# Mixture-of-experts block: four banks for the dense tile, its sums between the last rotations, W2's pieces inside it

## What is computed

```python
# layer 1: causal sums of exponentials, then a small gate
q, k = rope((x @ Wq.T).bf16), rope((x @ Wk.T).bf16)
scores = q @ k.T / 16
o = where(causal, exp(scores), 0).sum(-1)          # one number per row
x = layernorm(x + relu(o @ fc1_w.T + fc1_b) @ fc2_w.T + fc2_b)
# layer 2: three routers, 12 experts each, top 3 by softmax
xa = x @ P_w.T
C1, C2, C3 = (top3_softmax(xa @ U.T) for U in (U1, U2, U3))
h = gelu(sum(C1[:, e] * (x @ W1[e].T) for e in range(12)))
y = sum(C2[:, e] * (h @ W2[e].T) for e in range(12)) + C3 @ b2
x = layernorm(x + y)
```

## Time and profile before

| | us |
|---|---|
| median of 3 runs | 312.19 |
| lowest, highest | 311.31, 315.37 |
| the profiled execution | 311.88 |
| its span | 310.0 |
| PE busy | 273.9 (88%) |
| DVE busy | 249.2 (80%) |
| ACT busy | 164.0 (53%) |
| GpSimd (POOL) busy | 145.2 (47%) |

### The profile page before, as it was taken

The page is one execution under the profiler, slowest core; times in us unless marked ns, Lnnn a source line. Parts: engine busy times, 40 slices in busy tenths (PEclk is TensorE's granted clock), DMA queues, the critical chain, the costliest instruction groups (busy, mean ns, idle before and its releaser), DMA issues.

```text
span 310.0 us, 6417 instructions
## 1 busy us (share of the span) xinstructions
PE 273.9 (88%) x2028; PEld 196.9 (64%) x2030; DVE 249.2 (80%) x728; ACT 164.0 (53%) x341; POOL 145.2 (47%) x315
## 2 busy tenths in 40 slices
PE   7997999979791985999998998998998999899980
PEld 5443455434351553778887787787777878688870
DVE  0378689999979265488999999999999989987872
ACT  1247746755662116406854854854854956654430
POOL 0200017999999611225356256256256353374421
PEclk9999999997998598699999999999999999999997
DMA  8998999950000000000010010011000010110111
GB/s 235 416 393 246 169 169 207 146 71 0 0 3 1 0 0 0 2 2 19 19 30 23 18 30 26 17 27 30 18 24 30 20 32 26 32 32 21 37 34 38
DMA packets 19211, 20.50 MB, mean 66 GB/s; under 512 B 1620, under 2 KB 18408, under 8 KB 18664
## 3 DMA queue, kind: packets, MB, share of 16 engines
q1 hardware_dynamic: 18456, 19.13, 26.2%
q10 hardware_dynamic: 720, 0.93, 1.0%
HBM read 15.83 MB, written 4.19 MB: 65 GB/s over the span
## 4 chain that ended last, share of the span: by engine, by line
PE 40%; DVE 27%; POOL 14%; issue 8%; SPq 4%; DMA 4%; ACT 2%; DVEq 0%; POOLq 0%
PE bank L922 31%; DVE early L1287 9%; POOL W L406 5%; DMA W<-in_w2T 4%; POOL wtmp L403 4%; POOL W L405 3%; PE bank L760 2%; PE bank L808 2%; DVE early L1336 2%; SPq L333 2%; DVE st L1331 2%; DVE top L1156 2%; DVE x1T L1146 1%; DVE stats L1135 1%; DVE zrest L1171 1%
## 5 line engine op out<-in xcount | busy, mean ns | idle before, releaser
L922 PE MATMUL bank<-W,x1T 128*128 (+1 forms) x630 | 79.4, 281 | 8.5 <-DVE early L1287 5.0
L922 PE MATMUL bank<-W,early 128*128 (+1 forms) x630 | 74.5, 273 | 6.0 <-DVE early L1336 5.4
L922 PEld LDWEIGHTS bank<-W,x1T 128*128 128x128 f16 x630 | 61.4, 101 | 21.9 <-DVE early L1287 7.2
L1287 DVE SCALAR_TENSOR_TENSOR early<-bank,Csel,early 128x256 f32<-128x256 f32 x124 | 59.7, 482 | 14.2 <-PE bank L922 9.7
L922 PEld LDWEIGHTS bank<-W,early 128*128 128x128 f16 x630 | 59.5, 98 | 17.4 <-DVE early L1336 7.0
L760 PE MATMUL bank<-early,wqk 128*128 128x512 f32 x128 | 61.3, 611 | 2.4 <-ACT qk L551 1.8
L760 PEld LDWEIGHTS bank<-early,wqk 128*128 128x128 f32 x128 | 22.6, 193 | 22.9 <-issue 20.3
L672 ACT ACTIVATE early<-early 128x256 f32<-128x256 f32 x32 | 13.3, 417 | 45.0 <-DVE early L1287 44.7
L509 POOL TENSOR_SCALAR ve<-mv 128x1 f32<-128x1 f32 x32 | 7.3, 228 | 59.6 <-DVE mv L1332 58.9
L551 ACT ACTIVATE qk<-bank 128x512 bf16<-128x512 f32 x32 | 18.9, 594 | 30.6 <-PE bank L760 30.4
L1062 DVE TENSOR_TENSOR xcos<-qk,cb 128x1024 bf16<-128x1024 bf16 x16 | 12.0, 749 | 18.6 <-ACT qk L551 18.5
(11 more groups left out here) (117 smaller groups left out, 454.5 us busy)
## 6 DMA issues: line engine op xcount, KB each, us to landing
early<-in_xT SPq DMA_DIRECT2D x16, 256.0 KB, 7.8
xs<-in_x SPq DMA_DIRECT2D x32, 128.0 KB, 7.9
out<-early SPq DMA_DIRECT2D x32, 128.0 KB
W<-in_w1T SPq DMA_DIRECT2D x1, 2048.0 KB, 11.8
W<-in_w2T SPq DMA_DIRECT2D x1, 2048.0 KB, 12.4
W<-in_w1T SPq DMA_DIRECT2D x1, 1024.0 KB, 7.2
W<-in_w2T SPq DMA_DIRECT2D x1, 1024.0 KB, 14.1
wqk<-in_wqkT ACTq DMA_DIRECT2D x1, 512.0 KB, 3.7
```

What stands on the lines that cost most here:

```text
L922: mm = pe.matmul(where[:, 0:DIM], lhs(hx, c), w, start=(k == 0), stop=(k == 5))
L1287: dve.scalar_tensor_tensor(sums, bank[place[n]][:, 0:DIM], c, before, ALU.mult, ALU.add)\
```

## The change

The list place starts at bank 2 and goes round four banks from product 0. The last chunk's scores (7) get the banks HGT and MISC. On PE the products of tile 0 are dealt out anew between the last scores, and tile 1's first products (mixture(1, 0)) stand ahead of bias(0, 0), x1_transpose(2, 0) and bias(0, 1). On DVE the sums of tile 0 begin between rope(7, 0) and rope(7, 1), route_ids(0) ahead of them. W2's shared pieces (n = 4 to 7) leave chunks 6 and 7 on ACT and DVE and stand in the dense tile. On GpSimd weights_of(0) and C3_split(0) stand ahead of a W piece in chunk 7, and the last two pieces after select_of(0) and norm_scale(2). On ACT gelu(0) stands ahead of x1_high(2, 0) and bias_copy(0, 0), and begin(1) inside the dense tile.

```diff
@@ -173,6 +173,8 @@
         bank = [ps(f"bank{i}", [P, 512]) for i in range(8)]
         PROJ, SCORE, HGT, ROWS, XPOSE, MISC = (0, 1), (2, 3), 4, 5, 6, 7
         RING, HT = 4, 4
+        LAST_SCORE = (HGT, MISC)
         WARM = 28
         Z = GT * NR * NE
         KEPT = 10
@@ -284,7 +286,7 @@
 
 
 
-        place = [n % 2 if n < NE else n % RING for n in range(len(taker))]
+        place = [(n + SCORE[0]) % RING for n in range(len(taker))]
         before = [max((k for k in range(n) if place[k] == place[n]), default=None) for n in range(len(taker))]
 
         def last(t, m):
@@ -301,6 +303,9 @@
             n = 4 * (c - 3) + j
             if 0 <= n < len(EARLY):
                 aux(*EARLY[n])
+        def score_bank(n):
+            return bank[(SCORE if n < SPC * (NCH - 1) else LAST_SCORE)[n % 2]]
 
         def group(g):
             return 0 <= g < NG
@@ -490,14 +495,19 @@
             piece = 0
             for c in range(NCH):
                 for j in range(4):
+                    if (c, j) == (NCH - 1, 1):
+                        continue
                     early_aux(c, j, early)
+                    if (c, j) == (NCH - 1, 0):
+                        early_aux(c, 1, early)
+                        C3_split(0)
                     if c >= 4:
                         w_piece(piece)
                         piece += 1
-            select_of(0)
-            C3_split(0)
+                    if (c, j) == (NCH - 1, 2):
+                        select_of(0)
             norm_scale(2)
+            w_piece(piece)
 
             for i in range(NT + 2):
                 k, s = divmod(i, GT)
@@ -558,7 +568,7 @@
                 for s in (2 * part, 2 * part + 1):
                     n = SPC * c + s
                     act.wait_ge(score_done, n + 1)
-                    act.activation(expd[:, n % 2, 0:P * (T + 1)], bank[SCORE[n % 2]][:, 0:P * (T + 1)], ACT.Exp,
+                    act.activation(expd[:, n % 2, 0:P * (T + 1)], score_bank(n)[:, 0:P * (T + 1)], ACT.Exp,
                                    scale=float(DIM) ** -0.5, accum_out=o[:, c % 2, s:s + 1]).then_inc(exp_done, 1)
 
             def w_sum(q):
@@ -682,7 +692,7 @@
                 early_aux(c, 1, early)
                 if c == 2:
                     w_sum(1)
-                if c >= 4:
+                if c in (4, 5):
                     w_high(2 * (c - 4))
                 qk_copy(c, 2)
                 if c:
@@ -694,25 +704,28 @@
                 early_aux(c, 3, early)
                 if c in (1, 2):
                     w_sum(2 * (c - 1))
-                if c >= 4:
+                if c in (4, 5):
                     w_high(2 * (c - 4) + 1)
 
             x1_high(1, 1)
             begin(0)
+            w_high(NB)
             exps(NCH - 1, 0)
+            w_high(NB + 1)
             exps(NCH - 1, 1)
+            w_high(NB + 2)
+            C3T_copy(0)
             gate_relu(NCH - 1)
+            begin(1)
+            w_high(NB + 3)
             normed(2, 0)
-            C3T_copy(0)
             aux(0, 0, 0)
+            gelu(0)
             aux(0, 0, 1)
-            gelu(0)
 
             for i in range(1, NT + 2):
                 k, s = divmod(i, GT)
                 aux(k, s, 0)
-                if i == 1:
-                    begin(1)
                 if i <= NT:
                     t = i - 1
                     act.wait_ge(hT_done, t + 1)
@@ -768,7 +781,7 @@
                 for s in (2 * part, 2 * part + 1):
                     b, n = SPC * (c % 2) + s, SPC * c + s
                     wait(pe, exp_done, n - 1)
-                    sc = bank[SCORE[n % 2]]
+                    sc = score_bank(n)
                     for k in range(NC):
                         pe.matmul(sc[:, 0:P * (T + 1)], qr[:, c % 2, k, s, :], kr[:, k, b, 0:P * (T + 1)],
                                   start=(k == 0), stop=False, skip_group_check=True)
@@ -975,19 +988,25 @@
 
             x1_transpose(1, 1)
             route_count(0)
-            pe.wait_ge(qk_copied, 4 * NCH)
             pe.wait_ge(w_split, NE - NB)
             pe.wait_ge(wlo_done, NB)
-            first(range(0, 4))
+            first(range(0, 2))
+            pe.wait_ge(qk_copied, 4 * NCH)
+            first(range(2, 4))
             fc(2, 0)
+            first(range(4, 6))
+            pe.wait_ge(hgT_copied, NCH - 1)
+            pe.wait_ge(ids_done, 1)
             scores(NCH - 1, 0)
-            first(range(4, 7))
+            first(range(6, 8))
             fc(2, 1)
+            scores(NCH - 1, 1)
+            first(range(8, NE))
             C3_transpose(0)
-            scores(NCH - 1, 1)
-            first(range(7, NE))
             gate_transpose(NCH - 1)
             aux(0, 0, 0)
+            load_ids(0)
+            mixture(1, 0, lambda hx, c: x1T[:, 1, hx, c, :], range(TOPK))
             aux(0, 0, 1)
             pe.wait_ge(exp_done, SPC * NCH)
             pe.wait_ge(hgT_copied, NCH)
@@ -995,9 +1014,6 @@
             for i in range(1, NT + 2):
                 k, s = divmod(i, GT)
                 aux(k, s, 0)
-                if i == 1:
-                    load_ids(0)
-                    mixture(1, 0, lambda hx, c: x1T[:, 1, hx, c, :], range(TOPK))
                 if i >= 2:
                     t = i - 2
                     pe.wait_ge(hlo_done, t + 1)
@@ -1265,19 +1281,19 @@
                 if c == 3:
                     peak_pow()
                 early_aux(c, 2, early)
-                if c >= 4:
+                if c in (4, 5):
                     w_low(2 * (c - 4))
                 early_aux(c, 3, early)
+                if c == NCH - 1:
+                    break
                 rope(c, 1)
                 if c == 1:
                     w_amax(1)
                 if c == 2:
                     w_amax(2)
                     w_bound()
-                if c >= 4:
+                if c in (4, 5):
                     w_low(2 * (c - 4) + 1)
-            route_ids(0)
 
             def add_slot(t, m, j, sums, before):
 
@@ -1287,34 +1303,42 @@
                 dve.scalar_tensor_tensor(sums, bank[place[n]][:, 0:DIM], c, before, ALU.mult, ALU.add)\
                     .then_inc(slot_added, 1)
 
-            def first_mixture(t):
+            def first_mixture(t, js=None):
                 if t == 0:
                     dve.wait_ge(C_done, 1)
                 elif t % GT == 0 or t == 1:
                     dve.wait_ge(csel_done, t // GT + 1)
                 sums = acc1[:, t % 2, :]
-                for j in range(1, experts_of(t)):
+                for j in js or range(1, experts_of(t)):
                     if j == 1:
                         dve.wait_ge(acc_begun, t + 1)
                     else:
                         dve.wait_ge(slot_added, by_dve[t, 0, j] - 1)
                     add_slot(t, 0, j, sums, sums)
-                    if t == 0 and j == 3:
-                        fc_add(2, 0)
-                    if t == 0 and j == 5:
-                        fc_add(2, 1)
-                    if t == 0 and j == 7:
-                        norm_stats(2)
+            route_ids(0)
+            first_mixture(0, (1,))
+            rope(NCH - 1, 1)
+            first_mixture(0, (2, 3))
+            fc_add(2, 0)
+            first_mixture(0, (4,))
+            w_low(NB)
+            first_mixture(0, (5,))
             x1_low(1, 1)
-            first_mixture(0)
+            w_low(NB + 1)
+            first_mixture(0, (6, 7))
+            fc_add(2, 1)
+            norm_stats(2)
+            w_low(NB + 2)
+            first_mixture(0, range(8, NE))
+            w_low(NB + 3)
             aux(0, 0, 0)
+            first_mixture(1)
             aux(0, 0, 1)
             for i in range(1, NT + 2):
                 k, s = divmod(i, GT)
                 aux(k, s, 0)
-                if i == 1:
-                    first_mixture(1)
                 if i >= 2:
                     t, p = i - 2, i % 2
                     sums = y[:, t % 4, :]
```

## The result

The changed kernel takes 304.25 us (median of 4 runs, 301.98 to 304.85), beside 311.93 us for the kernel before on the same chip (311.31 to 315.37): ratio 0.973, 95% interval 0.967 to 0.979, so faster. The forecast was 303.4 us. The profiled execution took 304.48 us, its span 302.5.

A forecast was written before the change was run, and what follows sets the result against it. Hand-overs between TensorE and VectorE, not either engine, were taken to bound the stretch before 139 us. The second mixture, 10.3 us earlier, ends 8.55 us earlier at the lower clock: 311.88 - 8.5 = 303.4 us, range 300.0 to 309.0.

The forecast's parts named there:

- So PE has 6 us of room and the first slow period goes.: Dense tile: PE needs 15.8 us at full clock against DVE's 22, so the 98.7 to 108.7 us slow period disappears.
- Rival 2: Clock already falls in the dense tile, near 97 us, for 10 us: gain only 5.3, 306.6 us; chance 15%.
- rival 4: Dense tile's four w_high/w_low pairs hold DVE's sums 3.1 us each, and the clock drops: +9.0, 320.9 us; chance 4%.
- sum 1: Tile 0's first sum on DVE, between the last two rotations: starts at 94.5 us, takes 0.5, ends at 95.0.
- The two w_low gone from chunk 6 buy nothing there: Chunk 6 on DVE: sums of the exps still end at about 90.5 us, since they wait for GpSimd.
- Lower clock before 108 us makes the sum wrong: Stated sign of failure: PE at the lower clock before 108 us in the new profile would refute the forecast's sum.
- 7.3 us remain: From routing (zs) to tile 0's low half: 11.3 us before, less 4.0 for tile 1's 18 products.
- So it is covered, with 0.2 us to spare: ScalarE behind the dense tile: gelu 0 ends at 115.3 us, before x1_transpose(2, 0) ends at 115.5, so costs nothing.
- rival 3: Gelu 0's table switch costs more than its 1.28 us load and delays x1_high 1.1 us: 304.5 us; chance 8%.
- The clock gives some of it back: Behind the dense tile PE idles and its clock falls, slowing the second mixture: gain 8.55 us, not 10.3.
- Rival 1: Clock does not fall behind 110 us, so DVE paces the second mixture: gain 10.3, 301.6 us; chance 13%.
- The steady part: From the second mixture's end to the end of the span: unchanged work, 171 us long.

The follow-up runs named there:

- a2: Changed kernel with the dense tile put back on banks 0 and 1, everything else as changed: 307.59 us, ratio 0.984.
- a1: Changed kernel with tile 1's first products, their begin and sums put back behind the biases: 305.32 us, ratio 0.975.
- b3: Changed kernel with gelu 0 put back behind the two copies on ScalarE: 304.23 us, ratio 0.974.
- a4: Changed kernel with W2's four shared pieces (w_high, w_low) put back into chunks 6 and 7: 302.38 us, ratio 0.970.
- b2: Changed kernel with fc_add(3, 0) right behind tile 0's sums, plus 24 + 10 matmuls on zeros in the gaps behind the dense tile: 298.61 us, ratio 0.955.
- a5: Changed kernel with 22 matmuls on zeros added in chunk 7 ahead of scores(6, 0): 301.84 us, ratio 0.967.
- the repeat: The changed kernel measured again in another session, nothing changed: 302.98 us, ratio 0.969.
- b1: Changed kernel with fc_add(3, 0) directly behind tile 0's sums and the last w_low behind tile 1's sums: 300.61 us, ratio 0.960.
- a3: Changed kernel with 36 + 10 matmuls on zeros filling PE's gap behind the dense tile: 301.44 us, ratio 0.961.

## Why the prediction was right

The four intervals, each from one trace, take the gain apart:

| interval, us | gaps left | gaps filled |
|---|---|---|
| order before | 46.8 | 40.1 |
| changed order | 36.5 | 34.3 |

With the clock kept up in both, the new order is worth 5.8 us. Of the 10.3 us in the left column another 4.5 are the clock's: the slow periods cost the old order 6.7 us and the new one 2.2. This is the shape of the forecast (one slow period gone, one left). What of the 5.8 us belongs to which edit is known in part only: two banks are worth 3.6 (a2), tile 1's products 1.6 (a1), gelu 0 about 1.0 (b3), and W2's pieces took 1.5 away (a4), all with the clock's share in them. The sums between the rotations and the order on GpSimd, which the change is also made of, were never undone alone, and what they give is not shown.

**Its steps.**
- "So PE has 6 us of room and the first slow period goes." Right: no gap over 0.1 us from 95.0 to 111.7 us, clock 1.00. Without the two banks PE waits 1.35 and 1.97 us (a2). The gap of about 1 us ahead of the last scores is 0.35 us in b2 and 0.57 in a5, and is hidden where the slow piece makes PE late. Rival 2 did not come about; rival 4 neither, with 0.64 us of waiting in all.
- C done "at about 92.2 us" came at 93.10, and "sum 1" not at 94.5 but at 96.63, and this step failed. The late start is 1.7 us of it. The slow piece at 87.4 us, which left route_ids and the products waiting for PE, is 1.9: the first sum stands at 94.98 in the repeat and at 93.07 in a5, without it. Against these, the forecast was 1.4 us too late, for two reasons. "The two w_low gone from chunk 6 buy nothing there" was wrong: DVE's sums of the exps start at 89.06 in the repeat, at 90.03 before and at 90.08 in a4, which has the pieces back. And rope(7, 0) took 2.2 us where the sum had 3.4. "Lower clock before 108 us makes the sum wrong" was thus fulfilled, ahead of the dense tile. I had read gaps of PE only behind 92 us. The kernel before has one of 2.48 us ahead of scores(6, 0), where the clock held, and it was no part of my sum.
- From the first sum to zs: 17.0 us forecast (94.5 to 111.45), 16.0 measured. The w_low took 4.16 us together (forecast 4.4), and the last wait 0.64 (forecast 0.4). The rest is that the forecast adds whole durations, while neighbouring rows overlap: a sum put at 0.5 us takes 0.39 from its start to the next row's (101.38 to 101.77). The Trainium skill ("SBUF — State Buffer", section "SBUF: two separate sides") would have DVE's two-input instructions and GpSimd's reading ones exclude each other for their whole length. The rows agree in part: the same w_low takes 0.72 to 0.76 us beside a GpSimd with little to do and up to 1.34, in a4 1.53, beside a busy one. The dense tile's mean of 1.04 stayed under the 1.5 that I had kept as an end.
- "7.3 us remain" from zs to the low half: 7.6 (112.65 to 120.25), with PE's lower clock in it. That tile 1's 18 matmuls "leave the path" held (the prediction calls them, and the 72 of the second mixture, products; its 4.02/3 and 5.41/8 us a product count them rightly), but was priced too high: 4.0 us from their row, 1.6 in a1, because the slow period moves with them.
- "So it is covered, with 0.2 us to spare": x1_high waited 0.78 us for PE, not for gelu 0, so the cover was 0.8 us. The table load is followed by gelu 0.01 to 0.02 us after its end in the four traces that I read for it (the changed kernel's two, b1, b3), in b1 too, where x1_high waits for it. The drain of about 1.38 us in the Trainium skill ("ScalarE: Activation LUTs", section "What ACT_TABLE_LOAD costs") shows in none, and rival 3 falls. What the move saves is about 1.0 us, by the place of the second mixture in b3.
- "The clock gives some of it back": right in place (forecast 113 to 126, measured 114.8 to 125.0) and near in size (forecast 10.3 - 8.55 = 1.75 us, measured 2.3 in a3). The step "5.0 us after dense products began" fits this trace, counted from fc(3, 1) at 119.91, but is no rule: in b1 the same count gives 6.9 us (116.32 to 123.2), in a5 7.8. Rival 1 is what a3 shows when forced, 301.44 us against its 301.6, though the kernel before took 313.45 us in that session, so the gain is 12.0 us and not the rival's 10.3.
- The second mixture's end: 131.49 against 130.3 forecast, 0.9 us behind the low half forecast for its start and 1.8 measured, because fc(3, 1) in front of it took 2.07 us at the lower clock. The steady part came as said.

So the time was right by two errors that nearly cancel: a start 2.1 us too early, and an interval from first sum to end 0.9 us too long (35.8 against 34.9). Together they are the 1.1 to 1.2 us by which the profiled execution is over the forecast (304.48 against 303.4), and the median is nearer still. That they cancel is luck. And the gain over the kernel before is 7.7 us in the first session and 10.5 in the second, with 8.5 forecast, so an agreement within 1 us says no more than that the forecast lies between the two.

**Left open.** What decides between a slow piece at 87 us and none: gaps of 2.87 us or more had it in nine traces, but b2's of 2.89 us did not, and this was not tried beyond a5. Not tried either were the sums back behind both rotations with the rest as changed, and gelu 0 behind x1_high in b1's order, where the table load is on the path.
